# A linear-attention and FFN kernel: x loaded nine tiles ahead, its transpose moved, and both normalisations moved from VectorE to ScalarE

## The chip, the cores and the metric

The kernel runs on one core of a Trainium2 chip. The metric is device time in microseconds (us) from the start to the end of one execution. Before the change three runs gave 2465.79 us as the median (2458.34 to 2468.32).

## The reference

```python
# x: 8 x 2048 x 512 float32; 16 heads of 32; every W is 512 x 512
q = exp(split_heads(x @ Wq.T + bq));  k = exp(split_heads(x @ Wk.T + bk))
v = split_heads(x @ Wv.T + bv)
kv = cumsum(k[:, :, :, None] * v[:, :, None, :], axis=1)       # a state of 32 x 32 per head
k1 = cumsum(k, axis=1)
out = einsum('zsD,zsDd->zsd', q, kv) / sum(q * k1, axis=-1, keepdims=True)
x = layernorm(x + merge_heads(out) @ Wo.T + bo)                # first normalisation, eps 1e-5
h = ((x @ weight) @ aux_weight1) @ aux_weight2
x = layernorm(x + tanh(h + bias))                              # second normalisation
```

A layernorm here is `(r - mean) / sqrt(var + eps)` over the 512 features, with no gain and no offset.

## The kernel before

**Tiles and stages.** The 8 x 2048 rows of x are cut into 128 tiles of 128 rows. The batch index runs fastest: tile t belongs to batch t % 8, so each batch's running state is needed again eight tiles later. The three FFN matrices are multiplied into one, Wf, at the start. Every large product is made in three passes, from a high part and a low part of each operand (`xTH`/`xTL`, `oH`/`oL`, `x1H`/`x1L`): ScalarE writes the high part, GpSimd or VectorE the rest.

**Slots.** Each of the five engines runs its own program, a function `slot(c, k)` called for t = -8 to about 130. In slot k, TensorE works on several tiles at once. In order: the scores of tile k (L377, with `stateB` times q of tile k-1 ahead of it, L364), the numerator of k-1 (L389), the state update (L401), the denominator of k (L410, L411), a quarter of the Q and K projections of the four tiles of the next quad (12 matmuls each), the output projection of k-1 (`oH`, `WoH`: 12), the FFN of k-2 (`x1H`, `WfH`: 12) and V of k (12). `run_slots` writes the first and the last slots out and puts the middle ones, eight slots a turn, into a loop.

**What sets the order.** Nothing schedules at run time but semaphores: the order on an engine is the order in which its `slot` is written, and every cross-engine dependence is a wait in front of an instruction. All DMAs are issued by SyncE, also in the order of its `slot`.

**The path of x1, the first normalisation's output.** In VectorE's slot k: the residual r = `xres` + output projection (L712), its statistics (L714, L716); then GpSimd adds eps (`ve`, L779) and raises to the power -0.5 (`rstd`, L782); then VectorE writes x1 = (r - mean) * rstd (L724). SyncE stores x1 to DRAM (`x1_rows`, L288; the profile prints it as `x_rows`) and reads it back in another block order into `x1s` (L297, four DMAs). In its next slot VectorE turns the 32 x 32 blocks (L673), ScalarE takes the high part `x1H` (L533), VectorE the low part `x1L` (L682), and TensorE's FFN may start. The FFN shares a PSUM bank with the Q projection and so waits for ScalarE's `QT` (L538) as well.

**The other names.** L656 is the numerator times the reciprocal, L679 the reciprocal of the denominator (it waits for `oL`, made by GpSimd at L763, because it overwrites `o`), L698 the four scans that carry the running sum of k, L707 their product with q (`qk1`), whose low part GpSimd makes at L775. L720 adds the FFN bias, L558 is tanh, L786 adds x1 to it on GpSimd, L733 and L736 are the second statistics, L796 and L799 the second `ve` and `rstd`, L687 the second normalisation, one slot later. L730 turns the blocks of a tile of x, L568 and L792 split it. L563 copies V out of PSUM. L753 masks the scores.

**SyncE's slot.** x eight tiles ahead (it waits until GpSimd has split the tile before, since `xin` has two buffers), the output of k-3, the store and reload of K, the store of x1, the load of `xres` for k+1, and the reload of x1. At the start the weight loads stand between these slots: `load_wq_and_biases` behind slot -7, `load_wk` behind -5, the FFN's and Wv behind -4, Wo behind -2.

Of the kernel before, what the change touches and what calls it, by code (L numbers as in the profile page):

```python
# [26 lines left out]
def linear_attention_ffn_kernel(nc, x, wqT, wkT, wvT, woT, bq, bk, bv, bo, w, a1T, a2, bf, out):  # L27
# [16 lines left out]
    XIN = 2  # L44
    assert B == 2 * QUAD and NI >= 3

# [10 lines left out]
    with ctx:  # L57
# [3 lines left out]
        def sem(name):  # L61
# [40 lines left out]
        ve = sb("ve", [P, 2])  # L102
        rstd = sb("rstd", [P, 2])
        mhalf = sb("mhalf", [P, 1])

# [113 lines left out]
        def run_slots(engine, slot, ahead, behind, setup={}):  # L219

            for t in range(-ahead, B):
                slot(Chunk(t // B), t % B)
                if t in setup:
                    setup[t]()
            with nc.Fori(1, NI - 1, engines=(engine.engine,), hint_back_edge=True) as it:
                c = Chunk(it, engine)
                for k in range(B):
                    slot(c, k)
            for t in range(NT - B, NT + behind):
                slot(Chunk(t // B), t % B)  # L230
# [4 lines left out]
        def _(sp):  # L235
# [30 lines left out]
            def slot(c, k):  # L266
                if c.exists(k + 8):
                    n = k + 8

                    wait_before(sp, (xl_ready, c.count(n - 1)))  # L270
                    for j in range(HG):
                        sp.dma_start(xin[j * HD:(j + 1) * HD, n % XIN, :].rearrange("p (t f) -> p t f", t=HG),  # L272
                                     x_b[n % B, c.it + n // B, j]).then_inc(xin_loaded[n % B], 16)
                if c.exists(k - 3):
                    n = k - 3
                    wait_before(sp, (out_ready, c.count(n + 1)))
                    sp.dma_start(out_t[n % B, c.it + n // B], y[:, n % 2, :]).then_inc(out_stored[n % B], 16)
                if c.updates_state(k):
                    wait_before(sp, (k_turned, c.count(k + 1)))
                    sp.dma_start(k_rows, KS).then_inc(k_stored[k % B], 16)  # L280
                    wait_before(sp, (k_stored[k % B], c.dma_count(k)), (state_done, c.count(k)))
                    for j in range(HG):
                        sp.dma_start(Ktok[j * HD:(j + 1) * HD, :].rearrange("p (a c) -> p a c", a=HG),
                                     k_blocks[j]).then_inc(ktok_loaded[k % B], 16)
# [4 lines left out]
                if c.exists(k + 1):  # L289
                    if c.static() and c.it * B + k == -1:  # L290
                        sp.wait_ge(c_done, 1)
                    m = k + 1
                    sp.dma_start(xres[:, m % 2, :], x_t[m % B, c.it + m // B]).then_inc(xres_loaded[m % B], 16)
# [6 lines left out]
            run_slots(sp, slot, 8, 3, {-7: load_wq_and_biases, -5: load_wk, -4: load_ffn_weights_and_wv,  # L300
                                       -2: load_wo})
# [166 lines left out]
        def _(act):  # L468
# [38 lines left out]
            def slot(c, k):  # L507
# [32 lines left out]
                if c.reads_state(k):  # L540
                    wait(act, num_done, c.count(k))
                    wait(act, state_ready, c.count(k - 7))
                    for j in range(HG):
                        h = slice(j * HD, (j + 1) * HD)
                        last = nc.scalar.activation(stateB[h, :, h], state[h, k % B, :, :], ACT.Copy)
                    last.then_inc(stateb_ready, 1)
                if proj:
                    wait(act, kproj_done, c.count(k + 5))
                    wait(act, k_turned, c.quad_count(k - 4))
                    nc.scalar.activation(KT[:, ns, b, :], kproj_ps[:, :], ACT.Exp,  # L550
                                         bias=bcol[:, 1, b:b + 1]).then_inc(k_ready, 1)
# [4 lines left out]
                if ffn:  # L556
                    wait(act, z_ready, c.count(k - 1))
                    nc.scalar.activation(y[:, k % 2, :], y[:, k % 2, :], ACT.Tanh).then_inc(tanh_ready, 1)  # L558
                if att:
                    wait(act, v_done, c.count(k + 1))  # L560
                    wait(act, state_done, c.state_count(k - 1))
                    wait(act, num_done, c.count(k - 1))
                    nc.scalar.activation(V[:, k % 2, :], v_ps[:, :], ACT.Copy).then_inc(v_ready, 1)  # L563
                if c.exists(k + 8):
# [7 lines left out]

            run_slots(act, slot, 8, 2, {-7: split_wq, -5: split_wk, -4: split_aux, -3: split_a12,
                                        -2: split_wv_wf_wo, -1: free_staging})

        @block.vector
        def _(dve):
# [67 lines left out]
            def slot(c, k):  # L645
                att = c.exists(k)
                prev = c.exists(k - 1)
                ffn = c.exists(k - 2)
                fin = c.exists(k - 3)
                oflat = o[:, :, :].rearrange("p g q -> p (g q)")  # L650
                r = xres[:, (k - 1) % 2, :]
                yf = y[:, (k - 3) % 2, :]
                if prev:
# [7 lines left out]
                if c.updates_state(k):  # L661
# [4 lines left out]
                                        KT[:, (k // QUAD) % 2, :, cols].rearrange("p g (t q) -> p g t q", q=HD)  # L666
                                        ).then_inc(k_turned, 1)
                if ffn:
                    n = k - 2
# [4 lines left out]
                                        x1s[:, :].rearrange("p (t g f) -> p g t f", t=HG, f=HD)).then_inc(x1_turned, 1)  # L674
                if att:
                    wait(dve, den_done, c.count(k + 1))
                    wait(dve, oh_ready, c.count(k))
                    wait(dve, ol_ready, c.count(k))
                    nc.vector.reciprocal(oflat, den_ps[:, :]).then_inc(recip_ready, 1)  # L679
                if ffn:  # L680
# [3 lines left out]
                                            ALU.subtract).then_inc(x1l_ready, 1)  # L684
                if fin:
                    wait(dve, rstd2_ready, c.count(k - 2))
# [34 lines left out]
                if prev:  # L721
                    wait(dve, rstd1_ready, c.count(k))
                    wait(dve, y_ready, c.count(k - 2))
                    nc.vector.tensor_scalar(x1[:, (k - 1) % 2, :], r, mv1[:, 0:1], rstd[:, 0:1],  # L724
                                            ALU.subtract, ALU.mult).then_inc(x1_ready, 1)
                if c.exists(k + 8):
                    m = k + 8
                    wait(dve, xin_loaded[m % B], c.part_count(m))
                    xblocks = xin[:, m % XIN, :]
                    nc.vector.transpose(xblocks, xblocks).then_inc(x_turned, 1)  # L730
                if ffn:
# [5 lines left out]

            run_slots(dve, slot, 8, 3, {-7: split_wq, -5: split_wk, -4: split_aux,
                                       -3: split_a12, -2: split_wv_wf_wo, -1: add_bo})

        @block.gpsimd
        def _(pool):
# [3 lines left out]
            def slot(c, k):  # L746
# [30 lines left out]
                if prev:  # L777
# [16 lines left out]
                if c.exists(k - 2):  # L794
# [3 lines left out]
                    wait(pool, out_ready, c.count(k - 2))  # L798
                    nc.gpsimd.tensor_tensor(rstd[:, 1:2], ve[:, 1:2], mhalf[:, :], ALU.pow).then_inc(rstd2_ready, 1)  # L799

            run_slots(pool, slot, 8, 2)


# [34 lines left out]
```

## Time and profile before

| | |
|---|---|
| Median of three runs | 2465.79 us |
| The profiled execution: its time / its span | 2467.03 / 2465.3 us |
| TensorE (PE) busy | 2321.6 us, 94% |
| VectorE (DVE) busy | 1797.8 us, 73% |
| GpSimd (POOL) busy | 1314.3 us, 53% |
| ScalarE (ACT) busy | 1052.8 us, 43% |
| Mean granted TensorE clock | 0.992 |
| DMA queue q1 | 293712 packets, 30.9% of 16 engines' span |

Busy shares are averages over the whole program. A matmul's printed duration overlaps the next one's start, so distances on TensorE are read from start to start. In a row of order of time, `[3.61 <-DMA WK<-x_rows]` says that the engine stood idle for 3.61 us before this instruction and that the last thing it waited for was that DMA; `<-issue` names no releaser. `WK` is one SBUF tensor that holds y, x1, Ktok, KS, x1s and qk1. `G` are the PSUM banks of the projections, `SC` those of the scores, of which one also takes the turned x1.

### The profile page before, as it was taken

To read this page: it belongs to the slowest core of one execution; us is meant where nothing else is said; L and a number is where in the kernel's file an instruction comes from. 1 tells how busy PE (TensorE), PEld (TensorE's weight loads), DVE (VectorE), ACT (ScalarE), POOL (GpSimd) and SP (SyncE) were. 2 spreads that over 40 slices of the span, in tenths; PEclk is the share of its full clock that TensorE was granted. 3 is DMA by queue.
4 is the path that set the end of the run, shared out by engine and by line. 5 is a ranking of instruction groups with operands and counts; after the bars stand their busy time and mean duration, and the time that the engine had idled before them with its cause. 6 is when DMAs were issued, how large, how long until landed. Compare 5 with 4: busy or idle time off the path is not lost.

```text
span 2465.3 us, 58596 instructions
## 1 busy us (share of the span) xinstructions
PE 2321.6 (94%) x21040; PEld 1907.9 (77%) x21040; DVE 1797.8 (73%) x2710; ACT 1052.8 (43%) x2039; POOL 1314.3 (53%) x1669
## 2 busy tenths in 40 slices
PE   6999999999999999999999999999999999999985
PEld 5778878877877887777777877777777877777764
DVE  4677777777777777777777777777777777777664
ACT  3434444444444444444444444444444444444431
POOL 1455555555655555555555555554555555555553
PEclk9999999999999999999999999999999999999998
DMA  6233333333333333333333333333333333333211
GB/s 162 71 98 103 106 99 102 103 98 96 105 100 100 103 100 97 104 98 99 102 97 100 102 99 100 102 99 99 99 101 100 100 102 99 98 103 96 64 65 52
DMA packets 293918, 241.90 MB, mean 98 GB/s; under 512 B 32848, under 2 KB 225360, under 8 KB 293712
## 3 DMA queue, kind: packets, MB, share of 16 engines
q1 hardware_dynamic: 293712, 238.69, 30.9%
q8 instruction: 186, 3.05, 0.6%
q14 instruction: 20, 0.16, 0.0%
HBM read 139.99 MB, written 98.57 MB: 97 GB/s over the span
## 4 chain that ended last, share of the span: by engine, by line
PE 93%; issue 4%; DVE 1%; ACT 1%; DMA 0%; SPq 0%; POOL 0%; POOLq 0%; ACTq 0%; DVEq 0%
PE G L310 25%; PE G L312 24%; PE G L311 24%; PE SC L377 6%; PE G L389 5%; PE G L364 4%; PE G L410 2%; PE G L401 1%; PE G L411 1%; PE SC L310 0%; PE SC L312 0%; PE SC L311 0%; DMA QT<-wqT 0%; DVE o L656 0%; SPq L272 0%
## 5 line engine op out<-in xcount | busy, mean ns | idle before, releaser
L775 POOL TENSOR_TENSOR qk1L<-WK,qk1H 128x512 fp32r<-128x512 f32 x128 | 165.4, 1292 | 814.7 <-ACT qk1H L555 814.7
L679 DVE RECIPROCAL o<-G 128x512 f32<-128x512 f32 x128 | 424.9, 3320 | 2.8 <-PE G L411 1.4
L673 DVE STREAM_TRANSPOSE SC<-WK 128x512 f32<-128x512 f32 x128 | 93.0, 727 | 448.5 <-DMA WK<-x_rows 448.5
L753 POOL TENSOR_SCALAR_AFFINE_SELECT A<-A 128x512 f32<-128x512 f32 x512 | 314.4, 639 | 10.7 <-issue 6.6
L517 ACT ACTIVATE A<-SC 128x512 f32<-128x512 f32 x512 | 275.3, 591 | 61.1 <-PE G L389 59.7
L792 POOL TENSOR_TENSOR xTL<-xin,xTH 128x512 fp32r<-128x512 f32 x128 | 164.8, 1288 | 245.6 <-ACT xTH L568 245.5
L310 PE MATMUL G<-WfH,x1H 128*128 128x512 f32 x512 | 211.1, 412 | 83.4 <-issue 71.7
L555 ACT ACTIVATE qk1H<-WK 128x512 fp32r<-128x512 f32 x128 | 81.0, 633 | 469.6 <-DVE WK L707 469.6
L724 DVE TENSOR_SCALAR WK<-xres,mv,rstd 128x512 f32<-128x512 f32 x128 | 200.5, 1566 | 86.4 <-POOL rstd L782 86.4
L533 ACT ACTIVATE x1H<-SC 128x512 fp32r<-128x512 f32 x128 | 76.6, 599 | 374.0 <-DVE SC L673 374.0
L310 PE MATMUL G<-xTH,WqH 128*128 128x512 f32 x512 | 203.0, 396 | 28.7 <-POOL xTL L792 21.1
L310 PE MATMUL G<-WoH,oH 128*128 128x512 f32 x512 | 202.0, 395 | 11.7 <-issue 11.7
L310 PEld LDWEIGHTS G<-WfH,x1H 128*128 128x128 f32 x512 | 96.8, 189 | 144.9 <-issue 116.3
L698 DVE TENSOR_TENSOR_SCAN WK<-ones,k,KT 128x128 f32<-128x128 f32 x512 | 205.6, 463 | 0.0
L312 PE MATMUL G<-WfH,x1L 128*128 128x512 f32 x512 | 202.1, 395 | 0.0
L312 PE MATMUL G<-WoH,oL 128*128 128x512 f32 x512 | 201.6, 394 | 0.0
L311 PE MATMUL G<-WoL,oH 128*128 128x512 f32 x512 | 201.6, 394 | 0.0
L311 PE MATMUL G<-WfL,x1H 128*128 128x512 f32 x512 | 201.5, 394 | 0.0
L312 PE MATMUL G<-xTH,WqL 128*128 128x512 f32 x512 | 201.0, 393 | 0.0
L311 PE MATMUL G<-xTL,WqH 128*128 128x512 f32 x512 | 200.4, 391 | 0.0
L310 PE MATMUL G<-xTH,WkH 128*128 128x512 f32 x512 | 199.4, 389 | 0.0
L311 PE MATMUL G<-xTL,WkH 128*128 128x512 f32 x512 | 199.2, 389 | 0.0
(107 smaller groups left out, 5597.2 us busy)
## 6 DMA issues: line engine op xcount, KB each, us to landing
xin<-x SPq DMA_DIRECT2D x512, 64.0 KB, 1.9
xres<-x SPq DMA_DIRECT2D x128, 256.0 KB, 3.3
x_rows<-WK SPq DMA_DIRECT2D x128, 256.0 KB, 2.1
WK<-x_rows SPq DMA_DIRECT2D x512, 64.0 KB, 2.0
out<-WK SPq DMA_DIRECT2D x128, 256.0 KB, 2.1
k_rows<-WK SPq DMA_DIRECT2D x120, 256.0 KB, 2.3
WK<-k_rows SPq DMA_DIRECT2D x480, 64.0 KB, 2.0
QT<-wqT SPq DMA_DIRECT2D x4, 256.0 KB, 4.2
```

Of the source, the lines that this page charges most:

```text
L310: nc.tensor.matmul(out, statH(k), movH(k), start=(k == 0), stop=False)
L311: nc.tensor.matmul(out, statH(k), movL(k), start=False, stop=False)
L312: last = nc.tensor.matmul(out, statL(k), movH(k), start=False, stop=(k == NK - 1))
L377: last = nc.tensor.matmul(SC[:, j, g * P:(g + 1) * P], KT[h, s, g, cols], QT[h, s, g, cols], start=True, stop=True)
L389: last = nc.tensor.matmul(num_ps[h, g * P:(g + 1) * P], V[:, (k - 1) % 2, f0:f0 + HD], A[:, j, g, :], start=(g == 0 and not c.reads_state( ...
L517: nc.scalar.activation(A[:, j, :, :].rearrange("p g q -> p (g q)"), SC[:, j, :], ACT.Copy).then_inc(scores_out[j], 1)
L679: nc.vector.reciprocal(oflat, den_ps[:, :]).then_inc(recip_ready, 1)
L698: last = nc.vector.tensor_tensor_scan(qk1[:, g, :], ones[:, :].to_broadcast([P, P]), KT[:, nq, g, ncols], k1[:, nb, g:g + 1], ALU.mult, AL ...
L724: nc.vector.tensor_scalar(x1[:, (k - 1) % 2, :], r, mv1[:, 0:1], rstd[:, 0:1], ALU.subtract, ALU.mult).then_inc(x1_ready, 1)
L753: last = nc.gpsimd.affine_select(out=A[:, j, :, :], in_=A[:, j, :, :], compare_op=ALU.is_ge, fill=0.0, base=0, pattern=[[0, NK], [1, P]], ...
L775: nc.gpsimd.tensor_tensor(qk1L[:, :], WK[:, 7, :], qk1H[:, :].bitcast(F32), ALU.subtract).then_inc(qk1l_ready, 1)
L792: nc.gpsimd.tensor_tensor(halves[1], xin[:, m % XIN, :].rearrange("p (t g q) -> p g t q", t=HG, q=HD), halves[0].bitcast(F32), ALU.subtrac ...
```

## The change

It has three parts.

1. **x.** SyncE loads x nine tiles ahead, in place of eight, and starts one slot earlier (-9). In its slot the K store and reload come first, then x and the output; the reload of x1 now comes ahead of the load of `xres`, which waits for `x1_ready` (ScalarE now reads the buffer). VectorE turns tile k+8 ahead of the reciprocal and no longer near the end of its slot.
2. **x1's turn.** VectorE turns x1 behind the reciprocal instead of ahead of it.
3. **Normalisations.** GpSimd makes `shift = -mean * rstd` behind each `rstd` (a 128x1 instruction each), and ScalarE computes `rstd * r + shift` with `Identity`, scale and bias both taken from 128x1 operands. The second one stands between `stateB` and `KT` in ScalarE's slot, the first one between tanh and V. VectorE's two are gone.

The loop is also one turn shorter: eight more slots are written out at the end.

```diff
-                if c.exists(k + 8):
-                    n = k + 8
+                if c.updates_state(k):
+                    wait_before(sp, (k_turned, c.count(k + 1)))
...
+                if c.exists(k + 9):
+                    n = k + 9
                     wait_before(sp, (xl_ready, c.count(n - 1)))
...
+                if c.exists(k + 1):
+                    if c.static() and c.it * B + k == -1:
+                        sp.wait_ge(c_done, 1)
+                    wait_before(sp, (x1_ready, c.count(k)))
+                    m = k + 1
+                    sp.dma_start(xres[:, m % 2, :], x_t[m % B, c.it + m // B]).then_inc(xres_loaded[m % B], 16)
...
+            run_slots(sp, slot, 9, 3, {-7: load_wq_and_biases, -5: load_wk, -4: load_ffn_weights_and_wv,
                                        -2: load_wo})
@@ ScalarE
+                if c.exists(k - 3):
+                    n = k - 3
+                    wait(act, shift2_ready, c.count(n + 1))
+                    nc.scalar.activation(y[:, n % 2, :], y[:, n % 2, :], ACT.Identity, bias=shift[:, 1:2],
+                                         scale=rstd[:, 1:2]).then_inc(out_ready, 1)
...
+                if prev:
+                    n = k - 1
+                    wait(act, shift1_ready, c.count(n + 1))
+                    wait(act, y_ready, c.count(n - 1))
+                    nc.scalar.activation(x1[:, n % 2, :], xres[:, n % 2, :], ACT.Identity, bias=shift[:, 0:1],
+                                         scale=rstd[:, 0:1]).then_inc(x1_ready, 1)
@@ VectorE: removed
-                    nc.vector.tensor_scalar(yf, yf, mv2[:, 0:1], rstd[:, 1:2],
-                                            ALU.subtract, ALU.mult).then_inc(out_ready, 1)
...
-                    nc.vector.tensor_scalar(x1[:, (k - 1) % 2, :], r, mv1[:, 0:1], rstd[:, 0:1],
-                                            ALU.subtract, ALU.mult).then_inc(x1_ready, 1)
@@ GpSimd: behind each rstd (the second alike, with mv2 and column 1)
+                    wait_before(pool, (rstd1_ready, c.count(k)))
+                    nc.gpsimd.tensor_scalar(shift[:, 0:1], mv1[:, 0:1], rstd[:, 0:1], -1.0, ALU.mult,
+                                            ALU.mult).then_inc(shift1_ready, 1)
```

VectorE in a slot of the loop, before, from the K transpose to the second statistics. `WK<-KT` is the K transpose, `SC<-WK` the turn of x1, `xin<-xin` that of x:

```order
L665 STREAM_TRANSPOSE WK<-KT 128x4x4x32
L673 STREAM_TRANSPOSE SC<-WK 128x512
L679 RECIPROCAL o<-G 128x512
L682 TENSOR_TENSOR x1L<-SC,x1H 128x512
L687 TENSOR_SCALAR WK<-WK,mv,rstd 128x512
L698 SCALAR_TENSOR_TENSOR WK<-ones,k,KT 128x128 x4
```

And after the change, where x's turn has come in ahead of the reciprocal, x1's turn stands behind it and the second normalisation is gone:

```order
L677 STREAM_TRANSPOSE WK<-KT 128x4x4x32
L684 STREAM_TRANSPOSE xin<-xin 128x512
L689 RECIPROCAL o<-G 128x512
L695 STREAM_TRANSPOSE SC<-WK 128x512
L699 TENSOR_TENSOR x1L<-SC,x1H 128x512
L711 SCALAR_TENSOR_TENSOR WK<-ones,k,KT 128x128 x4
```

`x1L` now directly follows x1's turn, without the reciprocal between them.

ScalarE in the same slot after the change, from x1's high part to the split of x:

```order
L536 ACTIVATE x1H<-SC 128x512
L541 ACTIVATE QT<-G,bcol 128x512
L548 ACTIVATE stateB<-state 32x4x32 x4
L553 ACTIVATE WK<-WK,shift,rstd 128x512
L558 ACTIVATE KT<-G,bcol 128x512
L563 ACTIVATE qk1H<-WK 128x512
L566 ACTIVATE WK<-WK 128x512
L571 ACTIVATE WK<-xres,shift,rstd 128x512
L577 ACTIVATE V<-G 128x512
L582 ACTIVATE xTH<-xin 128x4x128
```

L553 (second normalisation) and L571 (first) are new; the other eight stand in the same order as before.

SyncE at the program's start, before (each `xin<-x` x4 is one tile of x, x8 two):

```order
L272 DMA xin<-x 32x4x128 x8
L245 DMA bcol<-bq 128x4
L246 DMA bcol<-bk 128x4
L247 DMA bcol<-bv 128x4
L242 DMA QT<-wqT 32x4x512 x4
L272 DMA xin<-x 32x4x128 x8
L242 DMA KT<-wkT 32x4x512 x4
```

And after:

```order
L281 DMA xin<-x 32x4x128 x12
L247 DMA bcol<-bq 128x4
L248 DMA bcol<-bk 128x4
L249 DMA bcol<-bv 128x4
L244 DMA QT<-wqT 32x4x512 x4
L281 DMA xin<-x 32x4x128 x8
L244 DMA KT<-wkT 32x4x512 x4
```

Three tiles of x are now issued ahead of Wq and five ahead of Wk, where it was two and four.

## Rows read from the trace of the kernel before

**Rows 1.** Waits over the whole span: who waited <- for what: us, times, longest.

```profile
DVE SC L673 <- DMA WK<-x_rows: 448.5, 128, 5.4
...
PE G L364 <- issue: 8.5, 13, 0.9
```

**Rows 2.** Busy time by stretch: us, then each engine; PE clock, DMA share, GB/s.

```profile
216.45:2368.01 2151.56, 2072.39 (x19119) 1709.51 (x19118) 1606.66 (x2425) 942.72 (x1852) 1187.77 (x1508) 1.00 0.31 99
```

**Rows 3.** TensorE in order of time (start, duration, idle before), one tile.

```profile
1206.44 1.05 PE L364 MATMUL G<-QT,stateB 128*128 128x128 f32 x8
...
1210.40 0.40 PE L310 MATMUL G<-xTH,WqH 128*128 128x512 f32 x1
...
1218.36 0.39 PE L312 MATMUL G<-WoH,oL 128*128 128x512 f32 x1
1219.39 0.47 PE L310 MATMUL G<-WfH,x1H 128*128 128x512 f32 x1 [0.65 <-issue]
...
1224.94 0.27 PE L364 MATMUL G<-QT,stateB 128*128 128x128 f32 x1
```

**Rows 4.** VectorE in order of time, the same tile and the next.

```profile
1214.79 0.73 DVE L673 STREAM_TRANSPOSE SC<-WK 128x512 f32<-128x512 f32 x1 [3.61 <-DMA WK<-x_rows]
1215.42 3.32 DVE L679 RECIPROCAL o<-G 128x512 f32<-128x512 f32 x1
1218.66 0.63 DVE L682 TENSOR_TENSOR x1L<-SC,x1H 128x512 fp32r<-128x512 f32 x1
1219.21 0.53 DVE L687 TENSOR_SCALAR WK<-WK,mv,rstd 128x512 f32<-128x512 f32 x1
...
1221.50 0.69 DVE L707 TENSOR_TENSOR WK<-WK,QT 128x512 f32<-128x512 f32 x1
...
1225.10 1.61 DVE L724 TENSOR_SCALAR WK<-xres,mv,rstd 128x512 f32<-128x512 f32 x1 [0.68 <-POOL rstd L782]
...
1228.17 0.69 DVE L656 TENSOR_TENSOR o<-G,o 128x512 f32<-128x512 f32 x1
...
1233.82 0.73 DVE L673 STREAM_TRANSPOSE SC<-WK 128x512 f32<-128x512 f32 x1 [4.14 <-DMA WK<-x_rows]
```

**Rows 5.** GpSimd, the same stretch.

```profile
1222.94 1.29 POOL L775 TENSOR_TENSOR qk1L<-WK,qk1H 128x512 fp32r<-128x512 f32 x1 [6.33 <-ACT qk1H L555]
1224.19 0.22 POOL L779 TENSOR_SCALAR ve<-mv 128x1 f32<-128x1 f32 x1
...
1225.16 1.27 POOL L786 TENSOR_TENSOR WK<-WK 128x512 f32<-128x512 f32 x1
1228.08 1.29 POOL L792 TENSOR_TENSOR xTL<-xin,xTH 128x512 fp32r<-128x512 f32 x1 [1.65 <-ACT xTH L568]
...
1230.79 1.29 POOL L763 TENSOR_TENSOR oL<-o,oH 128x512 fp32r<-128x512 f32 x1
```

**Rows 6.** ScalarE, the same stretch.

```profile
1225.14 0.60 ACT L563 ACTIVATE V<-G 128x512 f32<-128x512 f32 x1
...
1234.58 0.60 ACT L533 ACTIVATE x1H<-SC 128x512 fp32r<-128x512 f32 x1 [3.59 <-DVE SC L673]
1235.07 0.68 ACT L538 ACTIVATE QT<-G,bcol 128x512 f32<-128x512 f32 x1
```

**Rows 7.** SyncE's DMA issues, the same stretch.

```profile
1226.80 0.34 SPq L288 DMA_DIRECT2D x_rows<-WK  x1
```

**Rows 8.** SyncE's DMA issues at the program's start.

```profile
8.07 3.68 SPq L272 DMA_DIRECT2D xin<-x  x8
11.79 1.85 SPq L242 DMA_DIRECT2D KT<-wkT  x4
```

**Rows 9.** GpSimd at the start.

```profile
18.43 2.49 POOL L792 TENSOR_TENSOR xTL<-xin,xTH 128x512 fp32r<-128x512 f32 x2 [9.47 <-ACT xTH L568]
```

**Rows 10.** VectorE at the start.

```profile
21.25 2.29 DVE L606 TENSOR_TENSOR WkL<-KT,WkH 128x2048 fp32r<-128x2048 f32 x1 [3.05 <-ACT WkH L477]
```

**Rows 11.** ScalarE at the start.

```profile
29.50 0.69 ACT L550 ACTIVATE KT<-G,bcol 128x512 f32<-128x512 f32 x1 [2.25 <-PE G L312]
```

More of the change, by code:

```diff
@@ L44, in linear_attention_ffn_kernel @@
     XIN = 2
-    assert B == 2 * QUAD and NI >= 3
+    assert B == 2 * QUAD and NI >= 4
     x_t = x.rearrange("b (i p) d -> b i p d", p=P)
@@ L103, in linear_attention_ffn_kernel @@
         rstd = sb("rstd", [P, 2])
+        shift = sb("shift", [P, 2])
         mhalf = sb("mhalf", [P, 1])
@@ L128, in linear_attention_ffn_kernel @@
         scan_ready = sem("scan_ready")
+        shift1_ready, shift2_ready = sem("shift1_ready"), sem("shift2_ready")
         k1_ready = sem("k1_ready")
@@ L224, in run_slots @@
                     setup[t]()
-            with nc.Fori(1, NI - 1, engines=(engine.engine,), hint_back_edge=True) as it:
+            with nc.Fori(1, NI - 2, engines=(engine.engine,), hint_back_edge=True) as it:
                 c = Chunk(it, engine)
@@ L228, in run_slots @@
                     slot(c, k)
-            for t in range(NT - B, NT + behind):
+            for t in range(NT - 2 * B, NT + behind):
                 slot(Chunk(t // B), t % B)
@@ L266, in slot @@
             def slot(c, k):
-                if c.exists(k + 8):
-                    n = k + 8
+                if c.updates_state(k):
+                    wait_before(sp, (k_turned, c.count(k + 1)))
+                    sp.dma_start(k_rows, KS).then_inc(k_stored[k % B], 16)
+                    wait_before(sp, (k_stored[k % B], c.dma_count(k)), (state_done, c.count(k)))
+                    for j in range(HG):
+                        sp.dma_start(Ktok[j * HD:(j + 1) * HD, :].rearrange("p (a c) -> p a c", a=HG),
+                                     k_blocks[j]).then_inc(ktok_loaded[k % B], 16)
+                if c.exists(k + 9):
+                    n = k + 9
                     wait_before(sp, (xl_ready, c.count(n - 1)))
@@ L277, in slot @@
                     sp.dma_start(out_t[n % B, c.it + n // B], y[:, n % 2, :]).then_inc(out_stored[n % B], 16)
[L278 to L284, printed above, removed]
                 n = k - 1
@@ L288, in slot @@
                     sp.dma_start(x1_rows, x1[:, n % 2, :]).then_inc(x1_stored[n % B], 16)
[L289 to L293, printed above, removed]
                 if c.exists(n):
@@ L298, in slot @@
                                      x1_blocks[j]).then_inc(x1s_loaded[n % B], 16)
-            run_slots(sp, slot, 8, 3, {-7: load_wq_and_biases, -5: load_wk, -4: load_ffn_weights_and_wv,
+                if c.exists(k + 1):
[5 more added lines that the diff above has]
+            run_slots(sp, slot, 9, 3, {-7: load_wq_and_biases, -5: load_wk, -4: load_ffn_weights_and_wv,
                                        -2: load_wo})
@@ L571, in slot @@
                         ACT.Copy).then_inc(xh_ready, 1)
-            run_slots(act, slot, 8, 2, {-7: split_wq, -5: split_wk, -4: split_aux, -3: split_a12,
+            run_slots(act, slot, 8, 3, {-7: split_wq, -5: split_wk, -4: split_aux, -3: split_a12,
                                         -2: split_wv_wf_wo, -1: free_staging})
@@ L667, in slot @@
                                         ).then_inc(k_turned, 1)
+                if c.exists(k + 8):
+                    m = k + 8
+                    wait(dve, xin_loaded[m % B], c.part_count(m))
+                    xblocks = xin[:, m % XIN, :]
+                    nc.vector.transpose(xblocks, xblocks).then_inc(x_turned, 1)
+                if att:
+                    wait(dve, den_done, c.count(k + 1))
+                    wait(dve, oh_ready, c.count(k))
+                    wait(dve, ol_ready, c.count(k))
+                    nc.vector.reciprocal(oflat, den_ps[:, :]).then_inc(recip_ready, 1)
                 if ffn:
@@ L674, in slot @@
                                         x1s[:, :].rearrange("p (t g f) -> p g t f", t=HG, f=HD)).then_inc(x1_turned, 1)
[L675 to L679, printed above, removed]
                 if ffn:
@@ L684, in slot @@
                                             ALU.subtract).then_inc(x1l_ready, 1)
-                if fin:
-                    wait(dve, rstd2_ready, c.count(k - 2))
-                    nc.vector.tensor_scalar(yf, yf, mv2[:, 0:1], rstd[:, 1:2],
-                                            ALU.subtract, ALU.mult).then_inc(out_ready, 1)
                 n = k + 1
@@ L720, in slot @@
                     nc.vector.tensor_tensor(y[:, k % 2, :], ffn_ps[:, :], bfbc[:, :], ALU.add).then_inc(z_ready, 1)
-                if prev:
-                    wait(dve, rstd1_ready, c.count(k))
-                    wait(dve, y_ready, c.count(k - 2))
-                    nc.vector.tensor_scalar(x1[:, (k - 1) % 2, :], r, mv1[:, 0:1], rstd[:, 0:1],
-                                            ALU.subtract, ALU.mult).then_inc(x1_ready, 1)
[L726 to L730, printed above, removed]
                 if ffn:
@@ L736, in slot @@
                     nc.vector.bn_aggr(mv2[:, :], bnst[:, 1, :]).then_inc(stats2_ready, 1)
-            run_slots(dve, slot, 8, 3, {-7: split_wq, -5: split_wk, -4: split_aux,
+            run_slots(dve, slot, 8, 2, {-7: split_wq, -5: split_wk, -4: split_aux,
                                        -3: split_a12, -2: split_wv_wf_wo, -1: add_bo})
@@ L799, in slot @@
                     nc.gpsimd.tensor_tensor(rstd[:, 1:2], ve[:, 1:2], mhalf[:, :], ALU.pow).then_inc(rstd2_ready, 1)
+                    wait_before(pool, (rstd2_ready, c.count(k - 1)))
+                    nc.gpsimd.tensor_scalar(shift[:, 1:2], mv2[:, 0:1], rstd[:, 1:2], -1.0, ALU.mult,
+                                            ALU.mult).then_inc(shift2_ready, 1)
             run_slots(pool, slot, 8, 2)
```

2 lines of the change are left out of this document (removed).

## The prediction, made before the result was known

> **What bounds the kernel now.** I read the busy shares first: TensorE is busy 94% of the span, so at most a few per cent can be won, and only from its gaps. The second view is TensorE in order of time [rows 3]. A slot starts at 1206.44 with L364 and the next at 1224.94: 18.50 us. Within it everything runs back to back except one place. The last matmul of the output projection starts at 1218.36; matmuls of that kind follow each other every 0.227 us (35 steps from 1210.40 to 1218.36), so the FFN could start at 1218.59. It starts at 1219.39. The gap is 0.80 us, on average once per tile. The third view, VectorE in order of time, says why [rows 4]: `x1L` ends at 1219.29, and the FFN begins 0.1 later. `x1L` stands behind the reciprocal (3.32), that behind x1's turn (1214.79), and VectorE had stood idle 3.61 us before that turn for the reload of x1; over the program 448.5 us in 128 waits [rows 1].
>
> That closes a ring. x1's turn 1214.79, product `qk1` 1221.50, x1 written 1225.10 to 1226.71 [rows 4]; its store is issued at 1226.80 [rows 7]; the next turn is at 1233.82 [rows 4]. So 12.0 us of VectorE and GpSimd plus 7.0 us of DMA make 19.0 us here. From slot 8's reciprocal to slot 124's, 116 slots take 2151.56 us [rows 2], 18.55 each. The ring, not TensorE, sets that pace. TensorE's own slot is shorter: from slot start to FFN 12.15 (1206.44 to 1218.59), then FFN and V, 24 steps of 0.2274, 5.46: 17.61 us (today that part takes 5.55, because the first matmuls after a gap are slower) [rows 3].
>
> **The change, part by part.** Let N be the start of TensorE's slot and N' that of the next.
>
> *x1's turn behind the reciprocal.* The reciprocal no longer waits for the DMA. Instead the DMA has the reciprocal's 3.3 us to land in. What comes late next is GpSimd's `oL`, for which the reciprocal waits. Today `oL` starts 2.71 us after `xTL` (1228.08 to 1230.79) [rows 5].
>
> *The first normalisation.* From `qk1` at time a: `qk1L` a+1.44, `ve` a+2.69, and a+3.66 is where L786 starts today, rstd being done [rows 4, 5]. The new `shift` goes there. Its cost is not in the trace: at least 0.22 as `ve` [rows 5], at most 0.6 with a wait for its input; I take 0.22 and 0.06 for the signal. ScalarE's Identity from SBUF with two 128x1 operands isn't there either: lower bound V's copy without any, 0.60; one bias operand, on `QT`, makes it 0.68 [rows 6], a second as much again 0.76; upper bound the 1.61 of L724 [rows 4]. I take 0.8, nearest to the rows with an operand. So x1 is ready at a+4.75; today a+5.21 (1226.71). L724 takes 1.61 there, while L786 runs on GpSimd in the same stretch, against 0.53 for the same operation at L687, where GpSimd is idle [rows 4, 5].
>
> The Trainium skill ("ScalarE: Activation LUTs", Rules for kernel authors) speaks against this part: additions and products belong on VectorE. By rows 4, L687's 0.53 against my 0.8 agrees for the second normalisation, L724's 1.61 doesn't for the first. By that rule the move would add 0.27 us to the output's path, which nothing waits for; by the row it shortens x1's. The same page of the Trainium skill (What ACT_TABLE_LOAD costs) gives about 93 ns for each 128x1 operand; no row shows two of them together.
>
> *VectorE's load.* Gone are L687 (0.45 between the starts of `x1L` and the scans) and L724 (1.53). Added is one wait: `x1L` needs `x1H`, hidden under the reciprocal until now. `x1H` starts 0.76 after the turn and takes 0.60 [rows 4, 6]: `x1L` starts at turn + 1.41 and `qk1` 2.84 - 0.45 = 2.39 later [rows 4].
>
> *The new ring.* From a: `shift` a+3.66, L786 a+3.97, `xTL` a+5.24, `oL` 2.71 + 0.42 later (the second `shift`) a+8.4, reciprocal 1.3 later a+9.7, turn 3.24 later a+12.9, `x1L` a+14.35, next `qk1` a+16.7. The DMA comes in at a+4.75 + 0.1 + 7.0 = a+11.9, 1.0 us ahead of the turn, and without the `xres` load in between probably sooner. So the ring needs 16.7 us, less than TensorE's 17.61. TensorE becomes the bound.
>
> *Seen from TensorE.* VectorE takes the numerator at N+3.23 (1228.17 - 1224.94) [rows 3, 4]; `oL` can start at N+4.6, the reciprocal at N+5.9, the turn at N+9.2, `x1L` ends at N+11.2, `QT` (1.25 after the turn, 0.68 long [rows 4, 6]) at N+11.1. The FFN wants both at N+12.15: 0.9 us to spare. V, now behind the first normalisation on ScalarE, can be copied at N'+0.20 (1225.14) [rows 3, 6]; x1 is written by N+12.9+4.75 = N'+0.1. No conflict.
>
> *x ahead.* `xTL` waited for x's turn (1.65 idle before it [rows 5]); that wait goes, and with it 1.4 us on the way to `oL`. SyncE's K work now comes first: about 6 us of issuing and waiting, between the reload of x1 and the output; I cost it at nothing, since x1 is not due until N'+0.1.
>
> *Loop.* TensorE shows 13 gaps, 8.5 us in all, at L364 behind the loop's back edge [rows 1]. Today slack in the ring covers them; then they count.
>
> *The start.* This part costs. x has two buffers, so the third tile's load waits for the first tile's split, and it now stands ahead of Wq: 4 issues, 1.84 of the 3.68 us for 8 [rows 8]. Behind it come the biases and Wq, 7 issues, 3.3 us: issued by 13.2 instead of 8.07. Then tile 2's `xTL`, today at 18.43 + 1.25 [rows 9], comes at 24.8, the load of tile 4 waits for it, and only behind that load comes Wk: 26.6, where it is 11.79 today [rows 8]. Today's `WkL` ends 11.8 us after Wk's issue (21.25 + 2.29 - 11.79) [rows 8, 10], part of it in line behind other loads; so `WkL` is ready at 36 to 38.4 and the K projection ends at 39.5 to 44, against `KT` at 29.50 [rows 11], on which the remaining weight preparation hangs. The bounds are +5 (Wq alone) and +15; I take +12.
>
> *Sum.* 116 slots at 17.61 are 2042.8, plus 8.5 for the back edges: 2051.3, so -100.3. I give back 5 for late DMAs. The first FFN slots (2 to 7) have the same gap: -5. The last four have no Q and K projections, TensorE needs less than the ring, which falls from about 17.4 to about 16: -5. The drain holds both normalisations once more, each with a `shift`, +0.3 and +0.3: +1.2. Start +12. Profiled execution 2467.03 - 100.3 + 5 - 5 - 5 + 1.2 + 12 = 2374.9. The median lies 1.2 below that execution: 2373.7, I say **2373**.
>
> **Rivals.**
>
> *A part of the gap stays* (chance 0.22). `x1H`, `x1L` and `QT` all follow the turn now, and every 0.1 us that GpSimd's `oL` is late beyond the 0.9 spare reaches TensorE. For: GpSimd's chain is long and gets two more instructions with a wait each. Against: x's earlier turn gives it 1.4. If 0.4 per slot stays: 2373 + 116 x 0.4 = 2420; range 2392 to 2430.
>
> *The pace stays, the change doesn't do what it says* (0.07). SyncE reaches x1's store late, because K's store and reload and the output (which now waits for ScalarE) stand ahead of it; the DMA needs over 1 us more than in the ring above plus the 0.9 spare, and the ring is at 18.5 again. Against: K's work ends some 6 us before x1 is ready. Time: 2467 + 12 - 1.2 = 2478.
>
> *Slower* (0.07). The V copy waits on ScalarE behind the first normalisation, which waits for `shift`. L389 needs V at about N'+2.1. If x1 is written later than N'+1.4, TensorE itself waits, and everything behind the numerator with it: the ring numerator, `oL`, reciprocal, turn, `x1L`, `qk1`, `shift`, x1, V then closes through TensorE. By the rows above it takes 16.2 us. It decides from 17.61 on and makes the kernel slower from 18.55 on. At 19.0 it gives 2466 + 116 x 0.45 + 12 = 2530. Against it stand 1.4 us.
>
> **How the numbers follow.** My forecast (TensorE-bound) has 0.64; its own range is 2355 to 2392, from the start's +5 to +15 and a rest of up to 0.1 us per slot. Faster by over 0.5% (12.3 us, which a measurement of this kernel can just tell from none) is the forecast and the first rival, with a little of the cases between: 0.88; within 0.5% 0.05; slower 0.07. The range that leaves out no more than 2 in 10 is 2350 to 2425: it drops the two last rivals and the upper end of the first.
>
> **What would show it.** VectorE's wait for the reload of x1 falls from 448.5 us to near nothing; its largest wait becomes the one for `oL` before the reciprocal, with 0.65 us per tile for `x1H`. TensorE's gap before the FFN is gone in the middle of the program, slots follow each other every 17.6 to 17.7 us. The first K projection starts near 37 us, and slot 0's scores some 12 us later than today. The Identity rows read about 0.8. I am wrong if the FFN still waits in most slots, if a gap appears before L389 with V as the last thing to come, or if the start costs nothing.

## The result, and the profile after

The changed kernel takes **2481.63 us** as the median of five runs (2477.86 to 2482.19), against 2465.79 before: a ratio of 1.0064, 95% interval 1.0046 to 1.0082. It is 0.6% slower where I had forecast 3.8% faster.

The changed kernel's busy times and its chain that ended last:

```profile
PE 2331.3 (94%) x21040; PEld 1921.8 (77%) x21040; DVE 1574.2 (63%) x2454; ACT 1220.3 (49%) x2295; POOL 1386.0 (56%) x1925
...
issue 28%; PE 22%; POOL 20%; DVE 15%; ACT 13%; DVEq 1%; DMA 1%; SPq 0%; POOLq 0%; ACTq 0%
```

Before, that chain read:

```profile
PE 93%; issue 4%; DVE 1%; ACT 1%; DMA 0%; SPq 0%; POOL 0%; POOLq 0%; ACTq 0%; DVEq 0%
```

TensorE made up 93% of it and has 22% now; POOL, DVE and ACT together have 48%. The chain of before does not show the ring that the prediction found: the row of the FFN's gap names no releaser (`<-issue`, [rows 3]), and VectorE has 1% of the chain although the FFN starts 0.1 us after `x1L` ends.

Waits after the change (who <- for what: us in all, times, longest). L392 is the numerator (L389 before), L313 the FFN (L310), L367 `stateB` times q (L364):

```profile
DVE bnst L736 <- POOL WK L792: 314.5, 128, 3.5
...
DVE o L689 <- POOL oL L766: 195.9, 127, 4.0
...
DVE x1L L699 <- ACT x1H L536: 85.2, 128, 0.7
...
DVE WK L711 <- ACT KT L558: 74.4, 31, 2.5
...
PE G L392 <- ACT V L577: 52.1, 37, 2.0
...
PE G L367 <- issue: 7.3, 12, 1.0
...
DVE SC L695 <- DMA WK<-x_rows: 5.9, 2, 3.8
```

The wait that the change aimed at is gone: 448.5 us for the reload of x1 [rows 1] are 5.9. In its place stand the wait for `oL` and the one for `x1H`, both forecast. Two more cost time. The scans (L711 now) wait for `KT` 31 times, 2.4 us each, which the prediction did not have at all. TensorE waits for V 37 times at L392, which only the rival "slower" had. VectorE's largest wait, 314.5 us, is another one: the second statistics wait for GpSimd's sum of x1 and tanh. VectorE stands idle there where L724 and x's turn used to be; ktmid_vx below has the same wait (316.6 us) and is 100 us faster, so it is not what costs.

VectorE in an ordinary slot, which answers to [rows 4]:

```profile
1212.55 3.36 DVE L689 RECIPROCAL o<-G 128x512 f32<-128x512 f32 x1 [1.50 <-POOL oL L766]
1215.83 0.69 DVE L695 STREAM_TRANSPOSE SC<-WK 128x512 f32<-128x512 f32 x1
1217.19 0.69 DVE L699 TENSOR_TENSOR x1L<-SC,x1H 128x512 fp32r<-128x512 f32 x1 [0.67 <-ACT x1H L536]
...
1219.64 0.69 DVE L720 TENSOR_TENSOR WK<-WK,QT 128x512 f32<-128x512 f32 x1
...
1230.37 3.36 DVE L689 RECIPROCAL o<-G 128x512 f32<-128x512 f32 x1 [1.53 <-POOL oL L766]
```

GpSimd and ScalarE between `qk1` and the next reciprocal, which answer to [rows 5, 6]:

```profile
1223.51 0.27 POOL L787 TENSOR_SCALAR shift<-mv,rstd 128x1 f32<-128x1 f32 x1 [0.17 <-POOL rstd L785]
1223.73 1.27 POOL L792 TENSOR_TENSOR WK<-WK 128x512 f32<-128x512 f32 x1
1225.70 1.28 POOL L798 TENSOR_TENSOR xTL<-xin,xTH 128x512 fp32r<-128x512 f32 x1 [0.70 <-ACT xTH L582]
...
1228.95 1.29 POOL L766 TENSOR_TENSOR oL<-o,oH 128x512 fp32r<-128x512 f32 x1
```

```profile
1223.81 0.81 ACT L571 ACTIVATE WK<-xres,shift,rstd 128x512 f32<-128x512 f32 x1 [0.45 <-POOL shift L787]
1224.53 0.58 ACT L577 ACTIVATE V<-G 128x512 f32<-128x512 f32 x1
1225.01 0.62 ACT L582 ACTIVATE xTH<-xin 128x512 fp32r<-128x512 f32 x1
```

Reciprocal to reciprocal is 17.82 us: ordinary slots did come down from 18.55, to near the 17.61 forecast. Now one slot in four, the one that ends a quad. First VectorE, then ScalarE, then TensorE's gaps up to the next FFN:

```profile
1248.18 3.36 DVE L689 RECIPROCAL o<-G 128x512 f32<-128x512 f32 x1 [1.50 <-POOL oL L766]
1251.46 0.69 DVE L695 STREAM_TRANSPOSE SC<-WK 128x512 f32<-128x512 f32 x1
1252.81 0.69 DVE L699 TENSOR_TENSOR x1L<-SC,x1H 128x512 fp32r<-128x512 f32 x1 [0.67 <-ACT x1H L536]
1255.95 1.61 DVE L711 TENSOR_TENSOR_SCAN WK<-ones,k,KT 128x128 f32<-128x128 f32 x4 [2.44 <-ACT KT L558]
...
1269.17 3.36 DVE L689 RECIPROCAL o<-G 128x512 f32<-128x512 f32 x1 [1.90 <-POOL oL L766]
```

```profile
1252.18 0.60 ACT L536 ACTIVATE x1H<-SC 128x512 fp32r<-128x512 f32 x1 [4.79 <-DVE SC L695]
1252.68 0.68 ACT L541 ACTIVATE QT<-G,bcol 128x512 f32<-128x512 f32 x1
1253.25 1.25 ACT L548 ACTIVATE stateB<-state 32x128 f32<-32x128 f32 x4
1254.52 0.81 ACT L553 ACTIVATE WK<-WK,shift,rstd 128x512 f32<-128x512 f32 x1
1255.24 0.67 ACT L558 ACTIVATE KT<-G,bcol 128x512 f32<-128x512 f32 x1
```

```profile
1260.22 1.13 PE L367 MATMUL G<-QT,stateB 128*128 128x128 f32 x8 [0.90 <-issue]
...
1263.30 1.08 PE L392 MATMUL G<-A,V 128*32 128x128 f32 x32 [0.84 <-ACT V L577]
...
1274.59 0.47 PE L313 MATMUL G<-WfH,x1H 128*128 128x512 f32 x1 [0.95 <-DVE x1L L699]
```

`x1L` ends at 1253.50 and VectorE stands still for 2.44 us until `KT` is there; the next reciprocal is 20.99 us behind this one. Such slots take 20.3 us, or 21.0 where the loop's back edge (0.90 idle at L367) falls into them. TensorE waits behind all of it: for V (0.84) and for `x1L` (0.95).

From slot 8's reciprocal to slot 120's (231.47 to 2309.52) the mean is 18.55 us, exactly that of before (216.45 to 2293.76). Three slots at 17.8 and one at 20.3 or 21.0 are on average about 18.5. What the ordinary slots won, the fourth ones gave back. What is left is the start:

```profile
10.90 1.86 SPq L244 DMA_DIRECT2D QT<-wqT  x4
...
26.45 1.85 SPq L244 DMA_DIRECT2D KT<-wkT  x4
```

```profile
35.04 2.29 DVE L620 TENSOR_TENSOR WkL<-KT,WkH 128x2048 fp32r<-128x2048 f32 x1 [11.94 <-ACT WkH L480]
```

```profile
42.19 0.69 ACT L558 ACTIVATE KT<-G,bcol 128x512 f32<-128x512 f32 x1 [6.61 <-PE G L315]
```

Wk is issued at 26.45 and `KT` comes at 42.19, 12.7 later than in [rows 11]; slot 0's reciprocal starts at 91.16 where it was 78.17. Those 13.0 us account for most of the 15.8 between the medians.

The clock is not what costs in the slots. The mean granted clock was 0.984 in this execution and 0.992 before. Between 200 and 2250 us it fell nine times for some 3.5 us, to 0.50, which is 1.2 GHz in place of 2.4. One of these falls begins at 1041, after TensorE had stood idle 1.99 us for V, and the numerator there took 1.93 us in place of 1.08. But that slot, from reciprocal to reciprocal, took 20.32 us, like the same slots without a fall. Over slots 8 to 119 all slots that depart from the usual lengths add up to about 3 us.

### The profile page after: what moved, and what is told of

Read it like the earlier page. It is cut to its first block, busy times and chain, and to the rows that moved or that the text cites. A ratio compares the mean times of both kernels' runs of the same rounds, so it can differ in the third digit from the quotient of the medians.

```text
span 2480.4 us, 59115 instructions
## 1 busy us (share of the span) xinstructions
PE 2331.3 (94%) x21040; PEld 1921.8 (77%) x21040; DVE 1574.2 (63%) x2454; ACT 1220.3 (49%) x2295; POOL 1386.0 (56%) x1925
## 4 chain that ended last, share of the span: by engine, by line
issue 28%; PE 22%; POOL 20%; DVE 15%; ACT 13%; DVEq 1%; DMA 1%; SPq 0%; POOLq 0%; ACTq 0%
DVE WK L711 6%; PE G L313 6%; PE G L314 6%; PE G L315 6%; POOL oL L766 5%; POOL qk1L L778 4%; DVE SC L695 3%; DVE WK L720 3%; ACT qk1H L563 3%; POOL rstd L785 2%; ACT V L577 2%; POOL rstd L805 2%; ACT xTH L582 2%; ACT x1H L536 2%; PE G L392 1%
## 5 line engine op out<-in xcount | busy, mean ns | idle before, releaser
L736 DVE BATCH_NORM_STATS2 bnst<-WK 128x6 f32<-128x512 f32 x128 | 88.8, 694 | 314.5 <-POOL WK L792 314.5
L711 DVE TENSOR_TENSOR_SCAN WK<-ones,k,KT 128x128 f32<-128x128 f32 x512 | 205.9, 464 | 74.4 <-ACT KT L558 74.4
L313 PE MATMUL G<-WfH,x1H 128*128 128x512 f32 x512 | 209.2, 409 | 32.7 <-DVE x1L L699 28.0
L313 PE MATMUL G<-xTH,WqH 128*128 128x512 f32 x512 | 206.0, 402 | 26.4 <-POOL xTL L798 26.0
L313 PE MATMUL G<-WoH,oH 128*128 128x512 f32 x512 | 202.5, 396 | 12.0 <-issue 12.0
L313 PE MATMUL G<-xTH,WkH 128*128 128x512 f32 x512 | 200.0, 391 | 6.3 <-DVE WkL L620 6.3
L315 PE MATMUL G<-xTH,WkL 128*128 128x512 f32 x512 | 199.7, 390 | 0.0
L774 POOL TENSOR_TENSOR xres<-xres,cbc 128x512 f32<-128x512 f32 x128 | 165.4, 1292 | 61.4 <-DMA xres<-x 60.5
L313 PE MATMUL G<-WvH,xTH 128*128 128x512 f32 x512 | 199.2, 389 | 0.0
```

The source lines that it names most:

```text
L313: nc.tensor.matmul(out, statH(k), movH(k), start=(k == 0), stop=False)
L315: last = nc.tensor.matmul(out, statL(k), movH(k), start=False, stop=(k == NK - 1))
L711: last = nc.vector.tensor_tensor_scan(qk1[:, g, :], ones[:, :].to_broadcast([P, P]), KT[:, nq, g, ncols], k1[:, nb, g:g + 1], ALU.mult, AL ...
L774: nc.gpsimd.tensor_tensor(xres[:, k % 2, :], xres[:, k % 2, :], cbc[:, :], ALU.add).then_inc(xb_ready, 1)
```

## The experiments

Two theories stood against each other at the outset. **A**: the scans of every fourth slot wait for `KT`, and this has no slack to disappear in, because the ring is itself too long (the first normalisation stands ahead of V and xTH on ScalarE). **B**: what costs is V, late behind the first normalisation, so that TensorE waits at L392; that is my rival "slower".

Ratios are to runs of the kernel before on the same chip. The experiments ran on three chips, on which the kernel before had medians of 2462.02, 2462.57 and 2466.28 us, so a difference between the medians of two rows is uncertain by some 4 us. The mean slot is (start of slot 120's reciprocal - start of slot 8's) / 112 in the profiled execution.

| Kernel | Median us | Ratio, 95% interval | Mean slot | Ordinary / fourth slots |
|---|---|---|---|---|
| before | 2465.79 | 1 | 18.55 | mixed, 17.7 to 19.5 |
| changed | 2481.63 | 1.0064 (1.0046 to 1.0082) | 18.55 | 17.8 / 20.3, 21.0 |
| kt_first | 2417.11 | 0.9817 (0.9800 to 0.9833) | 18.05 | 17.8 / 18.4, 19.0 |
| vx_first | 2422.95 | 0.9841 (0.9825 to 0.9858) | 18.07 | 17.1, 17.6 / 19.6, 20.3 |
| dve_norms | 2373.35 | 0.9636 (0.9620 to 0.9652) | 17.71 | 17.1, 17.6 / 18.1, 18.9 |
| turn_ahead | 2381.81 | 0.9663 (0.9642 to 0.9683) | 17.78 | mixed, 16.7 to 19.3 |
| norm1_dve | 2405.59 | 0.9782 (0.9763 to 0.9800) | 17.94 | 17.1, 17.6 / 19.2, 19.9 |
| norm2_dve | 2426.56 | 0.9864 (0.9846 to 0.9881) | 18.11 | 17.7 / 19.1, 19.4 |
| ktmid_vx | 2381.80 | 0.9679 (0.9660 to 0.9698) | 17.73 | 17.6 / 17.6, 18.3 |
| start_only | 2467.44 | 1.0022 (1.0010 to 1.0034) | 18.56 | 17.8 / 20.3, 21.0 |
| x_only | 2437.18 | 0.9889 (0.9862 to 0.9917) | 18.10 | mixed, 16.9 to 20.2 |
| dve_start | 2359.69 | 0.9560 (0.9541 to 0.9579) | 17.72 | 17.1, 17.6 / 18.1, 18.9 |
| ktmid_vx_start | 2364.88 | 0.9583 (0.9564 to 0.9602) | 17.72 | 17.6 / 17.6, 18.2 |

### KT ahead: kt_first

```diff
@@ ScalarE's slot
-  x1H; QT; stateB; second normalisation; KT
+  x1H; QT; KT; stateB; second normalisation
```

> The changed kernel with one edit on ScalarE: KT's exponential directly behind QT's, ahead of stateB and of the second normalisation. Theory A (the scans of every fourth slot wait 2.44 us for KT, and the whole ring is late by that): KT comes 1.25 + 0.72 = 1.97 us earlier, the wait falls to about 0.5, 31 such slots give 61 us: about 2420. Rival B (what costs is V behind the first normalisation, 52 us of TensorE waiting at L392): KT has no part in it, 2475 to 2485.

Measured: 2417.11, 64.5 us less than the changed kernel. The row that decides:

```profile
DVE WK L711 <- ACT KT L546: 14.4, 31, 0.5
```

The scans' wait fell from 74.4 us to 14.4, 60.0 less, and the time by about as much. So the ring has no slack to absorb it, and rival B falls: V's own wait at L392 vanished too (52.1 to 3.2 us) although V stayed where it was. It was a consequence.

### V and xTH ahead: vx_first

```diff
@@ ScalarE's slot
-  tanh; first normalisation; V; xTH
+  tanh; V; xTH; first normalisation
```

> The changed kernel with V's copy and the split of x (xTH) ahead of the first normalisation on ScalarE. Theory A with its second half (the ring runs normalisation, V, xTH, xTL, oL, reciprocal, turn, x1L, qk1 and takes 17.8 us where TensorE needs 17.65): the ordinary slots fall from 17.81 to about 17.65 and the fourth ones from 20.3 to about 19.4, as the ring is 0.8 shorter, but the wait for KT stays: about 2438. Rival B (V alone is the cost): L392's wait goes and all 52 us with it, 2425 or less, and the fourth slots come down to the ordinary ones.

Measured: 2422.95, 58.7 less. The edit moves V and xTH together. But ordinary slots fell from 17.8 to 17.6, and in those of the changed kernel TensorE does not wait for V: from slot 8 on it does so once per quad, behind the fourth slot, and only once more. So what shortened them is xTH. The gain is larger than theory A had. The slots suggest why: the slack of the ordinary slots also takes up part of the wait for `KT`, which itself is unchanged (74.4 us), and the slot behind a fourth one runs in 17.1. The fourth slots stayed at 19.6 and 20.3, not down to the ordinary ones as B had it.

### The normalisations back on VectorE: dve_norms

```diff
@@ ScalarE
-  both Identity activations
@@ GpSimd
-  both shifts
@@ VectorE
+  tensor_scalar(yf, yf, mv2, rstd) behind x1L
+  tensor_scalar(x1, r, mv1, rstd) behind the FFN's bias
```

> The changed kernel with both normalisations back on VectorE (no shift on GpSimd), the rest of the change kept. Theory A: KT comes 0.8 earlier, V and xTH stand behind nothing, the ring is below TensorE's 17.65 in ordinary slots and near 18.0 to 18.3 in the fourth: about 2400, so moving the normalisations costs 80 us. Rival C (the DMA still sets the pace once VectorE carries its two normalisations again): slots of 18.3 to 18.5 throughout, 2450 to 2480.

Measured: 2373.35, a loss of 108 us for moving the normalisations, where I had expected 80. Its busy times:

```profile
PE 2293.9 (97%) x21040; PEld 1914.6 (81%) x21040; DVE 1812.4 (76%) x2710; ACT 1035.7 (44%) x2039; POOL 1334.0 (56%) x1669
```

```profile
DVE WK L705 <- ACT KT L553: 38.2, 30, 1.3
...
DVE SC L684 <- DMA WK<-x_rows: 6.5, 4, 2.9
```

TensorE is at 97% with VectorE at 76%, and the DMA plays no part. The scans still wait 1.3 us for `KT` in fourth slots, and it costs nothing: 18.1 and 17.1 are twice 17.6. Without its wait such a slot would take 18.1 - 1.3 = 16.8 us. That is an estimate of the ring's own length here, 0.8 below TensorE's 17.6; the other 0.5 us comes back in the next slot.

### x1's turn back ahead of the reciprocal: turn_ahead

```diff
@@ VectorE's slot
-  reciprocal; x1's turn; x1L
+  x1's turn; reciprocal; x1L
```

> The changed kernel with x1's turn put back ahead of the reciprocal, normalisations on ScalarE. Theory A: x1H, QT and KT run under the reciprocal, so the scans never wait for KT and all slots are alike; the ring through the DMA (x1 at a+4.75, 6.5 to 7.0 of DMA, turn, reciprocal, x1L, qk1) takes 17.6 to 18.1: about 2415. Rival B (V behind the first normalisation): the wait at L392 stays, 2470 to 2480.

Measured: 2381.81, 33 less than expected. With the turn ahead, `x1H`, `QT`, `stateB`, the second normalisation and `KT` all run under the reciprocal and `x1L`, and no scan waits for `KT`. VectorE waits for the reload of x1 again, but for 223.5 us and not 448.5:

```profile
DVE SC L690 <- DMA WK<-x_rows: 223.5, 124, 3.8
```

With x_only below, this makes a table of four, all with x nine tiles ahead. Normalisations on VectorE: 2437 with the turn ahead, 2373 with the turn behind. Normalisations on ScalarE: 2382 ahead, 2482 behind. So either the turn behind the reciprocal or the normalisations on ScalarE is worth having. It is the two together, in the order in which they were written, that lose.

### One normalisation at a time: norm1_dve, norm2_dve

```diff
@@ norm1_dve: only the first back on VectorE (and its shift gone)
@@ norm2_dve: only the second back on VectorE (and its shift gone)
```

> The changed kernel with only the first normalisation back on VectorE; the second stays on ScalarE ahead of KT, with its shift. Theory A in its present form (two causes add up: behind the first normalisation V and xTH lengthen the ring to 17.8, which leaves no slack for the 2.44 us that the scans wait for KT): without the first cause the ring has about 1 us of slack a slot and takes most of the wait of the fourth slots: 2375 to 2390. Rival E (it is the second normalisation, by putting KT 0.7 later, that costs): KT is as late as in the changed kernel, 2440 or more.

> The changed kernel with only the second normalisation back on VectorE, between x1L and the scans; the first stays on ScalarE ahead of V and xTH. Theory A: the ring keeps its detour and gets 0.45 us of VectorE on top, ordinary slots 18.2, the fourth ones about 19.4: 2440 to 2470. Rival E: KT comes 0.8 earlier, so most of the loss goes, under 2410.

Measured: 2405.59 and 2426.56; neither range held. With the first on VectorE the wait for `KT` stays at 74.4 us, 2.4 a time, and the slack takes up about half of it: a fourth slot and its successor take 19.2 + 17.1 = 36.3, 1.1 more than two ordinary ones (17.6 each). I had expected it to take up most. With the second on VectorE ordinary slots are at 17.7, not 18.2: I had added its 0.45 on VectorE and forgotten that GpSimd loses a `shift` of as much on the same ring. Both matter, theory A's two causes and rival E each in part: of the 108 us, the first alone gives 76 back and the second alone 55.

### Both causes gone by order alone: ktmid_vx

```diff
@@ ScalarE's slot
-  x1H; QT; stateB; second normalisation; KT ... tanh; first normalisation; V; xTH
+  x1H; KT; QT; stateB; second normalisation ... tanh; V; xTH; first normalisation
```

> The changed kernel, both normalisations on ScalarE, with both causes taken away by order alone: KT's exponential directly behind x1H (then QT, stateB, second normalisation), and V and xTH ahead of the first normalisation. Theory A: TensorE's 17.6 us a slot apart from the loop's back edge, 2365 to 2380, as with the normalisations on VectorE. Rival F (ScalarE's two extra instructions and GpSimd's two shifts cost by themselves): over 2395.

Measured: 2381.80, 2 us over its range's end and far from rival F's 2395. No wait of the scans for `KT` and none of TensorE for V is left in its list of waits. With `QT` now behind `KT`, TensorE waits for `QT` 12 times, 7.7 us in all. Of the 7.2 us between this span (2380.5) and that of dve_norms (2373.3), 3.3 lie behind the last reciprocal, outside the slots. VectorE, with 12 us per slot to do, and ScalarE and GpSimd each with two instructions more than before, all fit under TensorE.

### The start: start_only

```diff
-  {-7: load_wq_and_biases, -5: load_wk, -4: load_ffn_weights_and_wv, -2: load_wo}
+  {-8: load_wq_and_biases, -6: load_wk, -5: load_ffn_weights_and_wv, -3: load_wo}
```

> The changed kernel with the four groups of weight loads one slot earlier on SyncE (-8, -6, -5, -3), so that again two tiles of x stand ahead of Wq and four ahead of Wk. Nothing else. Slot 0's reciprocal comes 13 us earlier (78 where it is 91), the rest is the same: 2468 to 2469. If the start's delay were hidden by the ring, nothing: 2481.

Measured: 2467.44, 14.2 less than the changed kernel, and 0.2% above before.

### The first part alone: x_only

```diff
@@ both normalisations back on VectorE and both shifts gone, as in dve_norms
@@ x1's turn back ahead of the reciprocal, as in turn_ahead
```

> Only the first part of the change: x nine tiles ahead, its turn ahead of the reciprocal, SyncE's new order. x1's turn stands ahead of the reciprocal as before and both normalisations are on VectorE. Theory A: the ring through the DMA sets the pace as before the change, but the reload of x1 no longer stands behind the load of xres (5.9 us instead of 6.5 to 7.0) and x's turn is out of the way: 17.9 to 18.0 a slot, and the start costs its 13: about 2410. Rival G (x ahead brings nothing, it only costs the start): 2475.

Measured: 2437.18, a median of runs from 2428.3 to 2445.34, 27 over what I expected and 1.1% under before. Its mean slot is 18.10 in the profiled execution, the fastest of the four, 0.10 to 0.20 over what I expected: 11 to 22 us over 112 slots. In its trace SyncE issues the first reload of x1 as soon as the store has landed, here once 2.1 and once 4.1 us after it:

```profile
1229.28 0.35 SPq L290 DMA_DIRECT2D x_rows<-WK  x1
1231.37 2.60 SPq L294 DMA_DIRECT2D WK<-x_rows  x4
...
1247.49 0.35 SPq L290 DMA_DIRECT2D x_rows<-WK  x1
1251.61 1.74 SPq L294 DMA_DIRECT2D WK<-x_rows  x4
```

My sum used the typical store, 2.1 us to landing; the longest took 4.2, in the kernel before as well. A ring that holds the DMA can pay for each late one. That late stores make up the missing time is not shown, and why some are late stays open.

### What should be best: dve_start, ktmid_vx_start

> The changed kernel with both normalisations on VectorE and the weight loads one slot earlier on SyncE. Both effects were measured apart (2373.4 with the one; the other took 14.2 off the changed kernel, 2481.6 to 2467.4) and lie in different stretches, so they add: 2359. If TensorE-bound slots hid the start, 2373.

> Both normalisations on ScalarE, KT directly behind x1H, V and xTH ahead of the first normalisation, and the weight loads one slot earlier: 2381.8 less 14: 2368.

Each is dve_norms or ktmid_vx with the edit of start_only. Measured: 2359.69 and 2364.88, 0.7 over and 3 under what was expected. The start's gain is not hidden by slots that TensorE bounds: slot 0's reciprocal comes 14.0 and 14.9 us earlier than without it. The first is the fastest kernel here, 4.4% under before (0.9560, interval 0.9541 to 0.9579).

## Why the prediction was wrong, point by point

- **What bounds the kernel now** was right: dve_norms, which has parts 1 and 2, waits 6.5 us for the reload of x1 and takes 2373.35, 92 under before, and with the start mended (dve_start) 107 under the kernel before on its chip. The turn's move alone is worth 64 of it (x_only to dve_norms).
- **The start** (+12) was right, in its steps too: Wk is issued at 26.45 (forecast 26.6). It cost 13.0 in the trace and 14.2 between the medians of start_only and the changed kernel, which is 10 by their ratios. Of the small terms, the first FFN slots did not gain 5: from slot 0's reciprocal to slot 8's it took 140.3 us, 2.0 more than before. What lies behind the last reciprocal took 3.2 more, where 1.2 was forecast for the drain.
- **The reload of x1 in time, the Identity's price, the back edge** held: 5.9 us of waiting; the ScalarE row shows 0.81; the fourth slots with a back edge take 0.7 more.
- **"VectorE's load" failed**: "`qk1` 2.39 later". The scans for tile k+1 wait for `k_ready` of that tile's whole quad. In every fourth slot that is the `KT` of the same slot, and `KT` stands on ScalarE behind `x1H`, `QT`, `stateB` and the new second normalisation. Before, the reciprocal lay between x1's turn and the scans, and all of it ran beneath. The wait has no row before the change, and I looked for what is late next on VectorE only at `oL` and `x1H`. Price: 31 waits of 2.4 us; kt_first took 60.0 us of waiting and 64.5 us of time away.
- **"The new ring" failed by 1.1 us**: I let `xTL` follow L786 at a+5.24. In the trace, a being 1219.64, it starts at a+6.06. `xTH` has to come first, it stands behind V, and V behind the first normalisation, which waits for `shift`. So of the 1.65 us before `xTL` that "x ahead" let go whole, 0.70 stayed. I had checked this queue only for whether V was in time for TensorE. The second `shift` itself cost what I had put down (from the second `rstd` to the next mask 0.96 us, against 0.54 in norm2_dve, which has none). Summed from the rows: `oL` a+9.31, reciprocal a+10.73, turn a+14.01, `x1L` a+15.37, next `qk1` a+17.82, in place of 16.7. That is just above TensorE's need of 17.6, so nothing was left to take up the wait for `KT`. vx_first, which cuts this detour and leaves the wait for `KT` as it is, won 58.7 us.
- **The rival "slower"** named the right queue and the wrong point of decision: V at L392 does wait, 52 us, but as the result of the late ring. kt_first takes that wait from 52.1 to 3.2 us without moving V. The sign that I had named, a gap before the numerator with V last, did appear and pointed at the wrong cause.

Either error alone would have left the kernel faster: 2417 with the longer ring and little of the wait for `KT` (kt_first), 2423 with the full wait and the shorter ring (vx_first).

The wait for `KT` has no row in the trace of before, but all of its terms are there. The `KT` that belongs to the turn at 1214.79 [rows 4] is this one:

```profile
1217.89 0.69 ACT L550 ACTIVATE KT<-G,bcol 128x512 f32<-128x512 f32 x1
```

It ends 3.8 us after the turn, and 4.5 with 0.7 for the second normalisation ahead of it. The scans could start 2.0 after the turn (`x1L` at 1.41, and 0.6 from there to the scans, which is 1.05 less the 0.45 of L687). That gives a wait of 2.5 us; 2.44 were measured.

The Trainium skill's rule that products belong on VectorE ("ScalarE: Activation LUTs", Rules for kernel authors), which I had set against 0.27 us on a path that nothing waits for, picked the better side: dve_norms is 8.5 us below ktmid_vx. But the reason that the page gives, the cost per element, does not explain the loss here. With ScalarE's order mended, its 0.81 us against VectorE's 0.53 left the time nearly the same. The 100 us between the changed kernel and ktmid_vx come from the order on ScalarE alone, in which `KT` also went ahead of `QT` and `stateB`.

## What to carry to other kernels

An instruction that is moved to an engine with time to spare delays everything written behind it there, by its own duration and by whatever it waits for. List, for each instruction behind it, who waits for it, and do so for each slot of the period over which waits repeat (here four, a quad) and not for one typical slot. When a long instruction is taken out from between two others, what ran in its shadow has to be looked up in the semaphores, since the trace of before shows no wait for it. Slack decides what a wait costs. In dve_norms, with a ring some 0.8 us shorter than TensorE's slot, a wait of 1.3 us every fourth slot was free. In norm1_dve a wait of 2.4 us cost 1.1. In the changed kernel, with no slack, it was paid in full.

## What the runs showed that I had not expected

With no DMA in the ring, slots of one kind repeat to 0.02 us (17.80 to 17.82 over most of the changed kernel); with the DMA in it they scatter from 17.7 to 19.5. A VectorE tensor_scalar of 128x512 took 1.51 us in norm1_dve (at 1225.33), beside GpSimd's sum of x1 and tanh (L786 before, L788 there), and 0.54 alone in norm2_dve (at 1226.62), and dve_norms, which has both, is still faster than any kernel with a normalisation on ScalarE and the same start. TensorE is busy 97% there, so the extra microsecond did not set the pace.
